# Two output tiles used in turn in the last stage of a two-layer graph network, each with its own semaphore of stores

## The reference, cut to what matters

```python
h = x @ Wt.T + bt                                   # 4096 x 64
s = leaky_relu(h @ Wa.T + ba, negative_slope=0.2)   # one number for each node
scores = where(adj > 0, s, NEG)
w = softmax(scores, axis=1)
neighbor = w @ h
y = x + neighbor @ Wp.T + bp
out = gamma * (y - mean(y)) * rsqrt(var(y) + EPS) + beta
```

## Time and profile before

| what | value |
|---|---|
| median of 3 runs | 1278.1 us (1275.76 to 1278.79) |
| the profiled execution's own time | 1278.86 us |
| its span, first to last instruction | 1276.8 us |
| TensorE busy over the span | 1178.1 us (92%) |
| VectorE busy over the span | 1138.7 us (89%) |
| TensorE's mean granted clock | 0.976 |

### The profile page before, as it was taken

One profiled execution on the slowest core, in us unless ns is written; L12 is line 12 of the kernel. 1 busy time (PEld: TensorE's weight loads), 2 busy tenths in 40 slices (PEclk: granted clock), 3 DMA queues, 4 the chain that ended last, 5 costly groups with the idle time before them and its releaser, 6 DMA issues. The chain is left out here.

```text
span 1276.8 us, 31455 instructions
## 1 busy us (share of the span) xinstructions
PE 1178.1 (92%) x11639; PEld 332.7 (26%) x11639; DVE 1138.7 (89%) x1616; ACT 1052.6 (82%) x1194; POOL 982.9 (77%) x1028
## 2 busy tenths in 40 slices
PE   5888889999999999999999899999999998999976
PEld 2222222111111111111111111111111126775433
DVE  5989889999999999999999899999999994656756
ACT  4978889999999999999999899999999992441000
POOL 5867768999999989999998788888888872544222
PEclk8989899999999999999999999999999998999988
DMA  4332324754554455555445545555455457405870
GB/s 175 91 117 75 84 87 129 209 157 134 165 151 134 133 167 160 155 150 162 138 133 163 147 143 158 154 153 145 133 167 149 134 154 292 180 20 236 328 301 28
DMA packets 52672, 194.40 MB, mean 152 GB/s; under 512 B 6497, under 2 KB 20641, under 8 KB 42273
## 3 DMA queue, kind: packets, MB, share of 16 engines
q1 hardware_dynamic: 38944, 156.65, 34.5%
q0 software_dynamic: 9216, 33.56, 12.9%
q10 hardware_dynamic: 4352, 2.10, 0.6%
HBM read 114.69 MB, written 44.04 MB: 124 GB/s over the span
## 5 line engine op out<-in xcount | busy, mean ns | idle before, releaser
L1394 DVE SCALAR_TENSOR_TENSOR probs<-m,ps 128x512 f32<-128x512 bf16 (+1 forms) x1024 | 926.6, 950 | 30.9 <-PE ps L1586 14.8
L1291 ACT ACTIVATE probs<-probs 128x1536 f32<-128x1536 f32 x512 | 848.5, 1658 | 0.9
L1188 POOL TENSOR_TENSOR probs<-probs,m 128x512 f32<-128x512 f32 x512 | 634.7, 1270 | 118.9 <-ACT probs L1285 107.9
L1601 PE MATMUL ps<-probs,v_sb 128*17 128x512 f32 x4096 | 543.5, 603 | 0.0
L1586 PE MATMUL ps<-kq 32*128 32x512 bf16 x6144 | 429.3, 382 | 61.6 <-DVE probs L1394 33.8
L1285 ACT ACTIVATE probs<-ps 128x512 f32<-128x512 f32 x512 | 392.1, 766 | 33.3 <-PE ps L1586 32.1
L1586 PEld LDWEIGHTS ps<-kq 32*128 32x128 bf16 x6144 | 117.0, 93 | 580.0 <-ACT probs L1285 429.8
L1181 POOL TENSOR_SCALAR m<-adj_in 128x512 bf16<-128x512 int32 x256 | 192.9, 754 | 0.2
L1601 PEld LDWEIGHTS ps<-probs,v_sb 128*17 128x17 f32 x4096 | 68.2, 95 | 219.8 <-issue 208.3
L453 ACT ACTIVATE probs<-ps 128x512 f32<-128x512 f32 x8 | 4.8, 597 | 86.1 <-PE ps L798 84.1
L376 POOL TENSOR_TENSOR v_sb<-v_sb,cols 128x4 f32<-128x4 f32 (+1 forms) x9 | 8.8, 975 | 74.3 <-DVE v_sb L649 74.3
(11 more groups left out here) (140 smaller groups left out, 652.0 us busy)
## 6 DMA issues: line engine op xcount, KB each, us to landing
adj_in<-in_adj_t SPq DMA_DIRECT2D x64, 1024.0 KB, 5.7
mask_t<-m SPq DMA_DIRECT2D x64, 512.0 KB, 2.9
counts<-m POOLq DMA_DIRECT2D x64, 512.0 KB, 4.6
kq<-mask_t SPq DMA_DIRECT2D x16, 2048.0 KB, 9.7
counts_t<-counts SPq DMA_DIRECT2D x8, 512.0 KB, 7.4
attn_t<-acc_sb SPq DMA_DIRECT2D x16, 256.0 KB, 6.7
adj_in<-attn_t SPq DMA_DIRECT2D x8, 512.0 KB, 3.9
v_sb<-counts_t SPq DMA_DIRECT2D x8, 512.0 KB, 7.0
```

The costliest lines, as they stand in the source:

```text
L1188: nc.gpsimd.tensor_tensor(pr, pr, m01[:, (k // 2) % MRING, :], ALU.mult).then_inc(postmasked, 1)
L1291: nc.scalar.activation(pr, pr, ACT.Exp, scale=UNIT).then_inc(exped, 1)
L1394: nc.vector.scalar_tensor_tensor(out=pr, in0=m.to_broadcast([P, n, CH]), scalar=1.0, in1=ps[:, b:b + n, :], op0=ALU.subtract, op1=ALU.add)\
L1601: last = nc.tensor.matmul(ps[RT * hh:RT * hh + VW, 6 + g, :], v_sb[:, t, h * VW:(h + 1) * VW], probs[:, k % SLOTS, hh // 2, (hh % 2) * CH: ...
```

## The change

The output tile becomes two, used by even and odd chunks, and the semaphore of stores becomes two. L661 of chunk j now waits only for the two stores of chunk j-2 (from the third chunk on); SP waits at the end for both semaphores.

```diff
-        x2c, y, y_out = wb(SUB, D), wb(SUB, D), wb(SUB, D)
+        x2c, y, y_out = wb(SUB, D), wb(SUB, D), [wb(SUB, D), wb(SUB, D)]
...
-        out_made, out_stored = sem("out_made"), sem("out_stored")
+        out_made, out_stored = sem("out_made"), [sem("out_stored0"), sem("out_stored1")]
...
-            sp.wait_ge(out_stored, 32 * NC)
+            for u in range(2):
+                sp.wait_ge(out_stored[u], 16 * NC)
...
                     act.dma_start(out[at:at + CH // 2, :].rearrange("(s p) d -> p s d", p=P),
-                                  y_out[:, 2 * u:2 * u + 2, :]).then_inc(out_stored, 16)
+                                  y_out[j % 2][:, 2 * u:2 * u + 2, :]).then_inc(out_stored[j % 2], 16)
...
-                if j > 0:
-                    dve.wait_ge(out_stored, 32 * j)
+                if j > 1:
+                    dve.wait_ge(out_stored[j % 2], 32 * (j // 2))
                 for s in range(at.start, at.stop):
-                    last = nc.vector.scalar_tensor_tensor(out=y_out[:, s, :], in0=y[:, s, :], scalar=yrs[:, s:s + 1],
+                    last = nc.vector.scalar_tensor_tensor(out=y_out[j % 2][:, s, :], in0=y[:, s, :], scalar=yrs[:, s:s + 1],
                                                           in1=beta_r, op0=ALU.mult, op1=ALU.add)
```

## The result

The changed kernel takes 1267.89 us (median of 4 runs, 1265.67 to 1268.59), the kernel before 1277.44 us (4 runs, 1275.76 to 1278.79). The ratio is 0.9926, with a 95% interval of 0.9911 to 0.9941: 9.5 us less, and the interval lies clear of 0.3%. The forecast was 1268.9 us. Of all executions in this document one, of the kernel in which TensorE is kept busy, ran at a mean granted clock of 0.558, took 1846.96 us and is left out of its median.

What follows compares the result with a forecast made beforehand. TensorE was taken to set the pace, held once by a store through DVE. Pause 6.62 plus slow clock 2.55 gave 9.17 us: span 1276.8 to 1267.6, profiled 1269.7, median 1268.9 us; range 1266.0 to 1273.6 us.

Steps and rivals of the forecast that it cites:

- The pause: TensorE's stall before the projection of chunk 4, caused through DVE by chunk 3's store wait, goes: 6.62 us gained.
- The scaling back among the folds: L661 of chunk 3 starts 1.31 us after L653, at 1214.25, beside POOL's folds, and lasts 3.91 us, not 1.14.
- DVE's cover: In chunk 4, L601's sums allow L845 at 1220.49; TensorE arrives at 1221.21, so 0.72 us to spare.
- My estimate by the Trainium skill: L661 beside POOL's folds lasts at worst both folds plus its own work, 3.35 + 1.14 = 4.49 us.
- The slow clock: TensorE's lowered granted clock behind the stall goes too: 0.87 + 1.68 = 2.55 us, bounds 0 and 2.55 us.
- Chunk 2's wait: L661 of chunk 2 stops waiting for a store; a quarter microsecond on DVE, TensorE did not wait: worth 0.
- the end's second wait: SP waits for two semaphores in place of one at the very end, with nothing behind them: 0.
- the new places: The second tile pushes later scratch on; the second counts tile moves from `v_sb` to `m01`: 0.
- Chunk 5's cover: Chunk 3's second store, issued about 1218.1, lands at 1235.8 before chunk 5's L661 at 1238.04: 2.2 us of cover.
- (a): Rival: DVE is late in chunk 4 and the stall only shrinks, for example 4.8 us gained, 1273.3 us; chance 0.10.
- (b): Rival: the store wait moves to chunk 5; ending slower, 1282 us, chance 0.03; losing part of the gain, 0.04.
- (c): Rival: another condition, met at the same moment, also held L661, so the stall stays: 1278.1 us; chance 0.05.

Runs made afterwards that it cites:

- the larger sets: The changed kernel, unedited, measured again beside the kernel before: 1266.66 us (4 runs) against 1275.35 us (26 runs), then 1267.77 us (6 runs) against 1275.2 us (13 runs).

## Why the prediction was right

- **The pause, 6.62 us.** Right to 0.01 us in the profile: 8.29 us lie between the two projections of chunk 4, of which 1.66 were there already, which leaves 6.63. That it goes needs chunk 4's wait relaxed too, which the change does and the prediction puts no price on; relaxing chunk 3 alone showed it to be worth the whole gain.
- **The scaling back among the folds.** 3.92 us against 3.91 worked out, and 1.32 us after L654 against 1.31. DVE's cover before TensorE is 1219.54 - 1218.34 - 0.47 = 0.73 us against 0.72, and the run with more DVE work measured 0.74. My estimate by the Trainium skill (SBUF — State Buffer, section "SBUF: two separate sides"), 4.49 us for a loser that is blocked wholly, is 0.6 us above the 3.92 us measured here.
- **The slow clock, 2.55 us.** Real, as the run with TensorE kept busy shows: there the wait stays and the slow clock does not. Its size is 1.9 to 2.55 us in three traces, and the one that I had gave the upper end. I named no spread for it beyond 0 and 2.55.
- **The total, and what was luck in it.** With 6.62 and about 2 us the change is worth 8.6 us, not 9.2, and the larger sets have 7.4 to 8.7 us. The forecast of 1268.9 us is 1.0 us above the measured 1267.89, since two errors of opposite sign met: it started from 1278.1 us, the median of three executions, where the larger sets have 1275.2 to 1275.7 us, and it took off about 0.6 us too much. That the result's own pair of medians gave 9.5 us, so close to 9.2, is luck with its four executions of before.
- **Chunk 2's wait, worth 0; the end's second wait, worth 0; the new places, worth 0.** The run with the old wait confirms the last directly. The last low sums start at 1247.88, which with the 1.66 us is the 1249.5 forecast, so nothing else moved TensorE.
- **Chunk 5's cover.** I gave 17.7 us to land and 2.2 us of cover. Measured: the second store of chunk 3, issued about 1216.5, landed after 18.0 us, at 1234.5, and chunk 5's scaling began at 1236.38, 1.9 us later. With three tiles nothing changes.
- **What I did not see.** The trace of before held a third price, 1.66 us of slow clock behind the pause of chunk 1, that is there in some executions and not in others. It belonged in the text as a term of the spread between a profiled execution and a median, and would have moved nothing else.
- **The rivals.** (a) DVE is not late; its cover is as thin as said, and eats the first 0.7 us of any delay. (b) The wait does not move to chunk 5 with two tiles; with one relaxed wait it moves to chunk 4 at once. (c) The store was the releaser: with the same tiles, waiting for the newest stores or not is the whole difference between 1275.46 us and the changed kernel's 1266.66 us.

## What to carry to other kernels

When one buffer is waited for in a loop, the trace may show a long wait in one turn alone, because that stall clears the way for the turn behind. Here, relaxed in that turn only, the wait moved on by one and cost the same; so relax it for all turns. Cost such a stall on the engine that sets the pace, from the row where it could have gone on to the row where it did, and add the slow clock behind it. Then ask what slows the engine that feeds it: here VectorE's scaling ran beside GpSimd's folds in most chunks, which cost nothing where TensorE had no need to wait for VectorE, and 2.7 us in chunk 1, where it did. And take the time before from many executions: with four of them the gain came out at 9.5 us, with more at 7.4 to 8.7 us.

## What the runs showed of the hardware that I had not expected

- A store of 128 KB in runs of 512 B lands in 1.9 us when no load is under way. When loads of 2 MB keep the DMA engines full (415 to 424 GB/s), the first store of chunks 2 and 3 landed after 8.2 to 12.9 us, and the second, issued half a microsecond behind it, after 11.5 to 21.3 us, mostly 17 and more. The same code gave 12.0 us in one trace and 17.0 and 17.3 us in two others. Of the same bytes in runs of 1 KB the first landed after 7.2 and 7.3 us, the second after 11.0 and 12.3 us. That the two queues take turns piece by piece would fit; a larger cost of each small piece under load would too, and no run here separates them.
- The granted clock fell behind a pause of 2.7 us in two of nine traces, and behind one of 1.7 us in one of thirteen. Where it fell there, the sixteen high sums behind took 4.9 to 5.3 us in place of 3.6. Behind the pauses of 6.5 to 7.7 us it fell each time, in three of three traces, and they took 4.6 to 5.3 us.
- Twenty-eight matmuls whose results nobody reads made the kernel 1.3 us faster by the medians (0.5 to 3.4 us), by keeping the clock up through a wait.
